# First W1 copy a step earlier, group six's ranks in another bank, scatters paired: an audio-tower kernel on one core

## What is computed

```python
h = _L0_tok_ref(x, W, b, gamma, beta)          # patches of 5 frames -> relu -> batch norm: (32, 121, 128)
h = h + _L0_attn_ref(_layernorm(h), ...)       # 8 heads of 16, a bias per key column from the edge list
h = h + _L0_ffn_ref(_layernorm(h), ...)        # top-1 of 8 experts, each 128 -> 512 -> relu -> 128
```

## Time and profile before

| what | value |
|---|---|
| three runs | 281.76, 282.87, 283.83 us, median 282.87 |
| the profiled execution | 282.8 us, of which the span of its instructions is 281.1 us |
| TensorE matmul busy | 247.3 us (88% of the span), 2852 instructions |
| VectorE, ScalarE, GpSimd busy | 180.9, 165.8, 145.6 us |
| mean granted TensorE clock | 0.951 of full speed |

### The profile page before, as it was taken

One profiled execution on the slowest core, in us unless ns is written; L12 is line 12 of the kernel. 1 busy time (PEld: TensorE's weight loads), 2 busy tenths in 40 slices (PEclk: granted clock), 3 DMA queues, 4 the chain that ended last, 5 costly groups with the idle time before them and its releaser, 6 DMA issues.

```text
span 281.1 us, 8987 instructions
## 1 busy us (share of the span) xinstructions
PE 247.3 (88%) x2852; PEld 207.9 (74%) x2852; DVE 180.9 (64%) x679; ACT 165.8 (59%) x405; POOL 145.6 (52%) x275
## 2 busy tenths in 40 slices
PE   3999689999999999999998986975969559999693
PEld 3855466888887777878776755965969559999693
DVE  3896555678888788787788864663825225564352
ACT  3873355687676776766765664553536226776460
POOL 8001733344587776777776434475143744443444
PEclk9999999999999999999999997799798958999899
DMA  3110599000010111010110135123045423330000
GB/s 114 38 43 0 150 338 266 3 2 2 2 39 20 38 39 37 21 38 20 38 39 25 30 98 151 39 56 89 2 139 144 124 59 89 97 88 21 27 22 0
DMA packets 14462, 18.20 MB, mean 65 GB/s; under 512 B 3992, under 2 KB 10556, under 8 KB 14417
## 3 DMA queue, kind: packets, MB, share of 16 engines
q1 hardware_dynamic: 10976, 11.23, 14.1%
q0 software_dynamic: 3296, 6.00, 7.3%
q10 hardware_dynamic: 144, 0.41, 0.4%
HBM read 10.58 MB, written 7.54 MB: 64 GB/s over the span
## 4 chain that ended last, share of the span: by engine, by line
PE 67%; DVE 8%; issue 7%; another core or an unknown queue 6%; ACT 5%; POOL 3%; DMA 2%; ACTq 2%; POOLq 1%; SPq 0%; DVEq 0%
PE psS L1246 11%; PE psB L1146 9%; PE psS L1162 6%; PE psB L1236 5%; PE psO L1289 5%; PE psS L1172 4%; PE psO L1236 3%; PE psB L1130 3%; PE psU L1279 2%; DVE nmax L944 2%; PE psO L1267 2%; PE psU L1273 2%; PE psB L1152 2%; PE psB L1223 2%
## 5 line engine op out<-in xcount | busy, mean ns | idle before, releaser
L442 POOL DMA_INDIRECT out<-y_out,sidx x38 | 37.3, 980 | 47.1 <-DVE y_out L873 21.9
L1246 PE MATMUL psS<-xgT,W_tile 128*128 128x128 f32 x304 | 45.8, 300 | 2.7 <-ACT W_tile L557 2.6
L883 DVE TENSOR_SCALAR hT<-psS,b1T 128x128 f32<-128x128 f32 x76 | 23.3, 346 | 37.2 <-PE psS L1246 26.0
L944 DVE TENSOR_REDUCE nmax<-psS 121x8 f32<-121x968 f32 x32 | 37.2, 1164 | 14.6 <-PE psS L1172 13.2
L1246 PEld LDWEIGHTS psS<-xgT,W_tile 128*128 128x128 f32 x304 | 42.1, 214 | 3.3 <-issue 1.9
L609 ACT ACTIVATE PT<-psS 121x968 f32<-121x968 f32 x32 | 31.3, 978 | 17.3 <-DVE nmax L944 14.0
L572 ACT ACTIVATE hT<-psS,b1T 128x128 f32<-128x128 f32 x76 | 23.9, 364 | 29.5 <-PE psS L1246 21.3
L435 POOL DMA_INDIRECT region_d<-rows,pos x32 | 34.7, 1083 | 11.7 <-issue 11.4
L557 ACT ACTIVATE W_tile<-W_sb 128x512 f32 x38 | 23.9, 630 | 6.4 <-issue 3.7
L1236 PE MATMUL psB<-W_sb,hT 128*128 x168 | 25.6, 302 | 1.4 <-issue 1.4
L1236 PEld LDWEIGHTS psB<-W_sb,hT 128*128 128x128 f32 x168 | 23.7, 218 | 1.9 <-issue 1.7
(11 more groups left out here) (261 smaller groups left out, 545.0 us busy)
## 6 DMA issues: line engine op xcount, KB each, us to landing
xg<-region_d SPq DMA_DIRECT2D x38, 129.0 KB
W_sb<-in_L_ffn_W SPq DMA_DIRECT2D x1, 2048.0 KB, 9.8
region_d<-pads SPq DMA_DIRECT2D x1, 1032.0 KB, 6.7
out<-y_out,sidx POOLq DMA_INDIRECT x38
b_bc<-in_L_ffn_b SPq DMA_DIRECT2D x1, 512.0 KB, 5.1
region_d<-rows,pos POOLq DMA_INDIRECT x32
xs<-in_x ACTq DMA_DIRECT2D x1, 402.5 KB, 3.5
edge_i<-in_L_attn_edge_index SPq DMA_DIRECT2D x1, 64.0 KB, 3.8
```

Of the source, the lines that this page charges most:

```text
L442: pool.indirect_dma_start(out, bass.IndirectOffsetOnAxis(sidx[:, s:s + 1], 0), y_out[:, u, :], None, bounds_check=N - 1, oob_is_err=False) ...
L944: dve.tensor_reduce(nmax[0:L, :].rearrange("p (j c) -> p j c", c=HB)[:, :, HD + 1:HD + 3], score_half(0), AX.X, ALU.max, negate=True).then ...
L1246: ins = pe.matmul(psS[:, c // 2 * 2 + s % 2, c % 2 * 128:(c % 2 + 1) * 128], W1_tile[:, s % 2, c * 128:(c + 1) * 128], xgT[:, s % 2, :], s ...
```

## The change

The first W1 copy moves on ScalarE from behind `xgT_copy(1)` into step 31, between `turned_copy(27)` and `exponent(30)`. On TensorE `transpose_rows(0)` moves behind `scores_T(31)`. Group six: `experts(6)` moves from the end of VectorE's step 32 to ahead of `ffn_relu(0)` in the same step, with `expert_seen(6)` (before: step 34) behind it; `rank_rows(6)` moves from step 34 to step 33, writes to `psB[:, 1, 384:416]` in place of `psO`, and loses two waits; `rows_picked(6)` and `row_places(6)` move from step 34 to step 33, behind `first_sublayer(29)`; the wait for `r_pick` moves from ahead of `turn(31)` to ahead of `ffn_second(0)`, since that product writes the same bank. On GpSimd batch rows 20 and 21 are scattered in step 30, 22 and 23 in step 31, 24 in step 33, 25 in step 34, 26 in step 35 ahead of `rstd2(31)`, and 27 to 31 after it.

```diff
-            return first + (i if first < B else i // 2)
+            return first + (i if first < B - 2 else i // 2)
...
-            return psO if g < NG - 1 else psU
+            return psO[:, :] if g < NG - 2 else psB[:, 1, :] if g == NG - 2 else psU[:, :]
... (GpSimd)
                 if t == B + 3:
-                    for b in range(done, B - 6):
-                        scatter_rows(b)
-                    done = B - 6
+                    scatter_rows(B - 6)
+                    done = B - 5
                 if has(t, 4):
                     rstd2(t - 4)
-                while done < B and scatter_step(done) <= t:
-                    scatter_rows(done)
-                    done += 1
+                if t == B + 1:
+                    scatter_rows(B - 8)
+                if t == B + 2:
+                    scatter_rows(B - 7)
+                    done = B - 6
... (ScalarE)
                 if has(t, 4):
                     turned_copy(t - 4)
+                if t == B - 1:
+                    act.wait_ge(r_eid, 1)
+                    act.wait_ge(l_ffn, 48)
+                    W1_copy(0)
...
             xgT_copy(1)
-            act.wait_ge(r_eid, 1)
-            act.wait_ge(l_ffn, 48)
-            W1_copy(0)
... (VectorE)
-                if t == B + 2:
-                    rows_picked(NG - 2)
-                    row_places(NG - 2)
...
                     first_sublayer(t - 4)
+                if t == B:
+                    experts(NG - 2)
+                    expert_seen(NG - 2)
+                if t == B + 1:
+                    rows_picked(NG - 2)
+                    row_places(NG - 2)
...
                 ffn_relu(s, e)
                 e_next = tile_expert(s + 1)
-                if t == B + 2:
-                    expert_seen(NG - 2)
...
-                if t == B:
-                    experts(NG - 2)
... (TensorE)
-                    transpose_rows(0)
...
             scores_T(B - 1)
+            transpose_rows(0)
...
-                if t == B + 2:
-                    pe.wait_ge(s_oT, B - 1)
-                    pe.wait_ge(s_OTs, B)
+                if t == B + 1:
                     rank_rows(NG - 2)
...
                 if has(t, 3):
-                    if t == B + 2:
-                        pe.wait_ge(r_pick, NG - 1)
                     pe.wait_ge(s_OTs, min(t - 1, B))
                     turn(t - 3)
+                if t == B + 1:
+                    pe.wait_ge(r_pick, NG - 1)
                 ffn_second(s - 1, e)
```

## The result

The changed kernel takes 279.53 us (median of 16 runs, 277.5 to 282.02), the kernel before 282.79 us (16 runs, 280.39 to 284.62). The ratio is 0.9878, with a 95% interval of 0.9846 to 0.991: about 3.4 us faster. Forecast were 278.0 us (range 275.9 to 281.5) and a gain of 4.8 us. Medians are over all executions, while a ratio leaves out those over 1.5% above the fastest of their kernel, so the two need not agree.

A forecast was written before the change was run, and what follows sets the result against it. TensorE was taken to bound the kernel, by its 1.75 us pause ahead of the first expert product and half speed behind it. 2.08 + 2.02 + 0.66 = 4.76 us off 282.8 gave 278.0 us, range 275.9 to 281.5.

The forecast's parts named there:

- The front: TensorE up to tile 3's first product: 2.08 us from earlier start, 2.02 and 0.66 us behind it, together 4.76 us.
- signs that I had named for being right: W1 copy near 163.9, exponent 164.6, tile 0 near 168.4, clock 1.00 from 170 to 180, tile 3 near 177.4, logits awaited.
- signs of being wrong: Clock 0.50 after 172; VectorE-released wait over 0.6 us ahead of `ffn_second(0)`; new unknown-queue piece before 188, or sum beyond 19 us.
- The W1 copy: ScalarE, step 31: 0.34 us register load plus 0.63 us copy fit 0.95 us idle time; `exponent(30)` delayed 0.05 us.
- The transposition: TensorE, behind `scores_T(31)`: that product starts near 165.62 instead of 166.08, a gain of 0.23 us after the transposition.
- The clock: TensorE keeps full speed without the 1.75 us pause, saving 2.02 us from `output(29)` to `turn_back(31)` and 0.66 us to tile 3.
- Group six: VectorE, steps 32 and 33: earlier experts are hidden; `ffn_second(0)` waits 0.25 us for the new places, bounds 0 to 0.6.
- The scatters: GpSimd: moved batch rows are hidden, the last scatter ends 1.31 us earlier, worth nothing, at most 1.3 us more.
- Rival (1): Shorter scatter burst takes a stall with it: 4.8 plus 1.3 to 2.3 us gained, about 276.2 us; chance 0.08.
- Rival (5): Back-to-back scatters in steps 30 and 31 start two stalls of 3.3 us: slower, 284.6 us; chance 0.07.
- The shift running through to the end: From tile 5 on nothing is changed, so the 4.8 us gain was let run through to the end.
- rival (3): Gain given back later: one more unexplained stall or clock fall takes 3.3 from 4.8 us, 281.3 us; chance 0.10.

The follow-up runs named there:

- transposition back: Changed kernel with `transpose_rows(0)` at the end of step 31 again, ahead of `scores_T(31)`; 276.27 us, ratio 0.9784 to the kernel before.
- scatters back: Changed kernel with GpSimd's scatter stream as in the kernel before, in full; 281.69 us, ratio 0.9942 to the kernel before.
- W1 copy alone: Kernel before with only the first W1 copy moved into step 31 on ScalarE; 282.0 us, ratio 0.9918 to the kernel before.
- both back: Changed kernel with GpSimd's scatter stream and `transpose_rows(0)` both as in the kernel before; 280.15 us, ratio 0.9886 to the kernel before.
- all together: Changed kernel with old scatter stream and transposition place, tile 0's expert register loaded early, output scatters spread; 276.53 us, ratio 0.9738 to the kernel before.
- W1 copy with transposition: Kernel before with the first W1 copy in step 31 and `transpose_rows(0)` behind `scores_T(31)`; 281.16 us, ratio 0.9874 to the kernel before.
- register early: Changed kernel with tile 0's expert number loaded into its register ahead of `turned_copy(27)`; 279.66 us, ratio 0.9881 to the kernel before.
- pairs alone: Kernel before with only batch rows 20 to 23 scattered two per step from step 30; 284.08 us, ratio 1.0007 to the kernel before.
- outputs spread: Changed kernel with GpSimd's output scatters catching up by one in four tiles, not all at once; 275.78 us, ratio 0.9778 to the kernel before.
- filler: Changed kernel with one unread 256-column TensorE product in the pause ahead of `scores_T(31)`; 279.76 us, ratio 0.9898 to the kernel before.

## Why the prediction was right or wrong

The forecast of the time and its sign held, and in part by luck. The front, meant to bring all of the 4.76 us up to tile 3, brought 1.25 and 2.00 us. The tiles 3 to 8 beside the scatters, whose move was put at nothing, brought another 2.6 and 4.2 us, and part of that was lost again. Of the signs that I had named for being right, the first profile has the wait for group seven's logits (0.76 us) and no pause directly ahead of tile 0's first product. None of the times is met, even if the 0.53 us by which `scores(31)` starts later in this execution are taken off, and the clock is at 0.50 after 172, one of my signs of being wrong. The other signs of being wrong, a wait ahead of `ffn_second(0)` and a new unexplained piece before 188, did not come.

*The W1 copy: right in its effect, wrong in a term.* Alone it puts tile 0's product 1.91 us earlier and gives 2.3 us by the ratio. The mis-sized term is the register load: 0.34 us, read where it partly lay under the operations ahead of it. Behind `turned_copy(27)` it leaves ScalarE idle for 0.94 to 0.95 us in every profile that has it there, so the load and the copy take some 1.57 us and `exponent(30)` is half a microsecond late. I had named a bound of 0.35 us and taken 0.05. Being behind a wait is not the whole reason: in the kernel before, a later load also stands behind an operation that had waited, and costs 0.38 us.

```profile
207.87 0.28 ACT L564 ACTIVATE xgT<-psB 128x128 f32<-128x128 f32 x1 [1.02 <-PE psB L1223]
208.52 0.63 ACT L557 ACTIVATE W_tile<-W_sb 128x512 f32 x1 [0.38 <-issue]
```

*The transposition: wrong in sign, as far as the profiles go.* The step said that `scores_T(31)` would start at 165.62 and gain 0.23 us. It starts behind a late exponent instead, and the work that lay in this pause now stands behind it. With the transposition back, tile 0 comes at 7.38 instead of 9.27 and 7.80 (changed kernel), at 6.69 instead of 8.30 (scatters back), and without it at 6.68 instead of 8.30 (W1 copy alone). Where the clock held in both (7.38 against 7.80) the difference is 0.42 us; in the others half speed adds to it. The ratios say so in two of the three comparisons (0.9784 against 0.9878 and 0.9858, 0.9886 against 0.9942) and the opposite in the third (0.9918 against 0.9874); no interval settles it clearly.

*The clock: the certainty wrong.* Half speed stretches a tile's first product to 1.91 us as I had it, but I took it that the clock holds without the 1.75 us pause. In the four profiles with the W1 copy moved and the transposition left (W1 copy alone, transposition back, both back, all together) it held there, and tile 3 of both back came at 15.82 us against the 15.56 us that the working gives (177.42 - 161.86). The sum for the front was thus off by 0.26 us, for a kernel that isn't the changed one. With the transposition moved, the clock fell in four profiles (changed kernel, W1 copy with transposition, register early, scatters back) and held there in the other three. The Trainium skill, as cited in the prediction ("TensorE: Matmul & The Clock Gate", Part 1), has activity as what releases the slow clock. These falls come in a stretch where TensorE has several pauses, which agrees; neither my rows nor the rule as cited told which of two like stretches would do it.

*Group six: right.* Alone it is worth nothing (0.998), and the wait for `r_pick`, put at 0.25 us, is not there: in the changed profile `ffn_second(0)` at 176.98 follows `turn(30)` directly. Its earlier places are what lets batch rows 24 to 26 be scattered earlier.

*The scatters: wrong.* The step was "I cost it at nothing". From tile 3 to tile 8 the kernels with GpSimd's old stream need 16.6 to 18.1 us (before 17.69, W1 copy 18.05, with transposition 17.69, group six 17.52, pairs 18.09, scatters back 16.55, both back 17.79, all together 17.83). The ones with the whole new stream need 13.5 to 15.1 (changed 15.08 and 13.54, transposition back 13.89, outputs spread 13.49, register early 13.47, filler 14.48). The clock does not explain it: without a fall between these tiles it is 16.55 against 13.5 to 14.5, with one 17.5 to 18.1 against 15.08. Pairs alone, with the old end, belong to the slow group, so it is the end of the stream that does it. Whether batch rows 24 to 27 going earlier or the run of six being broken up counts was not separated. What this is worth in the whole time is less sure: 2.4 us by scatters back, nothing by the W1 copy with transposition, whose 0.9874 is the changed kernel's ratio; part of it is given back behind tile 11. Rival (1) named this mechanism, at 0.08 and on top of a full front. It came in place of the front. Rival (5), that scatters back to back cause stalls, has the same mechanism: it holds for the pair of step 30, at 0.7 us where I had put 3.3.

*The shift running through to the end: wrong by about 2 us.* At tile 11 the changed kernel is 5.0 and 6.8 us ahead, at the end 3.1 and 4.8. Meanwhile the two unexplained pieces beside the later run of output scatters grew by 2.1 us in the first profile, and the spread of these scatters leaves only two smaller ones, 4.7 us in all; rival (3) was such a loss, at 3.3 us.

## What to carry to other kernels

When an unexplained piece lies beside a run of indirect DMAs, look at how many follow one another before looking at who is late. Spreading a run here was worth about as much (2.3 to 2.8 us) as shortening the chain of products by 2 us (2.3). A duration read behind another instruction of the same engine may be only what stuck out: leave room for more before it is moved into an idle stretch. And work that an engine does while it waits should not be moved behind the wait, above all when what it waits for may have become later.

## What was not expected of the hardware

Where GpSimd issues indirect DMAs in a row, the other engines were released late by TensorE. With two back to back, VectorE and ScalarE were released 0.7 us late. Beside runs of six, ScalarE waited twice, 3.6 and 1.5 us in scatters back; beside runs of four once, 3.52 and 2.87 us in the changed kernel. Beside the nine output scatters from 212.36 to 223.5 us of the changed kernel stand the unexplained pieces of 5.42 and 5.69 us. By TensorE's records, whose ends are modelled, the products were done long before. The pair of step 30 was put in and taken out (pairs alone, scatters back), and the spread of the outputs, with no other edit, cut the last two from 11.1 to 4.7 us; that the scatters are the cause is shown for these. By which path they act is not shown by any run here and stays open, and so does how long a run can be before it costs. Busy DMA engines alone are not it: inside the last two pieces there are microseconds without any DMA traffic while TensorE, VectorE and ScalarE stand nearly idle (the last two numbers are DMA share and GB/s):

```profile
218.00:219.00 1.00, 0.00 (x0) 0.00 (x0) 0.29 (x1) 0.00 (x0) 0.70 (x2) 0.74 0.00 0
...
223.00:224.00 1.00, 0.00 (x0) 0.00 (x0) 0.00 (x0) 0.00 (x0) 0.54 (x1) 0.50 0.00 0
```

The first load of an expert's number leaves ScalarE idle for 0.95 us behind `turned_copy(27)`, a later one 0.38 us behind a copy that had waited; why the first takes longer is open. A version with the new end of the scatter stream, the transposition back, scatters 20 to 23 one per step and the outputs spread suggests itself, and was not tried.
